# Routed tiles of an expert layer: register reads, gather buffers and result buffers of the tile loop

## What is computed

```python
def _L0_ffn_ref(x, router_w, w1, w2):
    ...
    logits = xt @ router_w.T
    probs = jax.nn.softmax(logits, axis=-1)
    top_w, top_i = lax.top_k(probs, K)
    e_sel = jnp.max(top_i, axis=-1)
    def step(out, inp):
        idx, W1e, W2e = inp
        y = jax.nn.silu(xt @ W1e) @ W2e
        mask = (e_sel == idx)[:, None]
        return (jnp.where(mask, y, out), None)
    ...
x = x + _L0_ffn_ref(_layernorm(x, axis=-1)[None], L0_ffn_router_w, L0_ffn_w1, L0_ffn_w2)[0]
```

## Time and profile before

| what | us |
|---|---|
| median of 3 runs | 2702.45 |
| lowest and highest run | 2683.28, 2715.99 |
| span of the profiled execution | 2680.6 |
| TensorE busy in it | 2412.7 (90%) |
| GpSimd busy in it | 799.4 (30%) |
| routed stage, from the first transpose to the issue of the last addition | 2532.82 to 2671.07 |

### The profile page before, as it was taken

The page is one execution under the profiler, slowest core; times in us unless marked ns, Lnnn a source line. Parts: engine busy times, 40 slices in busy tenths (PEclk is TensorE's granted clock), DMA queues, the critical chain, the costliest instruction groups (busy, mean ns, idle before and its releaser), DMA issues. The chain is left out here.

```text
span 2680.6 us, 44378 instructions
## 1 busy us (share of the span) xinstructions
PE 2412.7 (90%) x16483; PEld 1631.1 (61%) x16483; DVE 1387.3 (52%) x2865; ACT 800.5 (30%) x1093; POOL 799.4 (30%) x562
## 2 busy tenths in 40 slices
PE   5889899999999999998993999999998899999476
PEld 2676767676766666665562566666664556666354
DVE  6575858574676766765211444444440444444333
ACT  3333333332374554743111222222220011111132
POOL 2134444444555555555553000000000000000265
PEclk9889999999999999999996999999998999999698
DMA  9974545554313223123214566665646754444185
GB/s 388 396 252 126 163 93 158 138 149 111 95 1 60 25 35 59 0 60 77 54 1 134 212 218 217 217 217 217 217 156 222 248 179 168 166 163 147 44 159 112
DMA packets 160992, 392.23 MB, mean 146 GB/s; under 512 B 74064, under 2 KB 81082, under 8 KB 151260
## 3 DMA queue, kind: packets, MB, share of 16 engines
q1 hardware_dynamic: 77196, 299.90, 32.5%
q0 software_dynamic: 72864, 61.03, 13.0%
q10 hardware_dynamic: 10800, 29.50, 2.9%
HBM read 226.03 MB, written 169.81 MB: 148 GB/s over the span
## 5 line engine op out<-in xcount | busy, mean ns | idle before, releaser
L364 PE MATMUL pair<-arena 128*128 128x384 f16 (+2 forms) x5760 | 908.5, 319 | 26.9 <-SPq L353 7.4
L1761 PE MATMUL pair<-arena 128*128 128x384 f16 x4900 | 823.1, 328 | 66.9 <-issue 40.7
L675 POOL DMA_INDIRECT cells<-arena x392 | 640.7, 1634 | 641.7 <-DMA cells<-arena 467.5
L364 PEld LDWEIGHTS pair<-arena 128*128 128x128 f16 (+1 forms) x5760 | 568.2, 99 | 353.0 <-issue 30.1
L1761 PEld LDWEIGHTS pair<-arena 128*128 128x128 f16 x4900 | 476.8, 98 | 379.0 <-issue 59.6
L1586 PE MATMUL pair<-arena 128*128 128x256 f32 x600 | 172.5, 422 | 19.3 <-ACT arena L780 19.3
L705 POOL DMA_INDIRECT slots<-arena x25 | 29.2, 1167 | 517.0 <-DVEq L1460 501.0
L1597 PEld LDWEIGHTS pair<-arena 128*128 128x128 f32 x1200 | 157.1, 198 | 23.8 <-ACT arena L805 18.9
L1597 PE MATMUL pair<-arena 128*128 128x66 f32 x1200 | 157.3, 280 | 14.4 <-ACT arena L805 14.4
L1131 DVE SCALAR_TENSOR_TENSOR arena<-arena 128x256 f16<-128x256 f32 x392 | 161.8, 482 | 4.7 <-DVE arena L1056 4.4
L699 POOL TENSOR_TENSOR arena<-arena 128x128 f32<-128x128 f32 x24 | 12.2, 507 | 502.5 <-DMA arena<-cells 481.1
(11 more groups left out here) (194 smaller groups left out, 2266.6 us busy)
## 6 DMA issues: line engine op xcount, KB each, us to landing
cells<-arena POOLq DMA_DIRECT2D x25, 1600.0 KB, 11.8
arena<-cells SPq DMA_DIRECT2D x25, 1600.0 KB, 9.4
ahl_dram<-arena SPq DMA_DIRECT2D x25, 1600.0 KB, 12.8
arena<-ahl_dram SPq DMA_DIRECT2D x25, 1600.0 KB, 7.9
arena<-in_x SPq DMA_DIRECT2D x70, 384.0 KB
arena<-key_dram SPq DMA_DIRECT2D x28, 896.0 KB
split_w<-arena SPq DMA_DIRECT2D x32, 384.0 KB
arena<-split_w SPq DMA_DIRECT2D x32, 384.0 KB, 6.7
```

The source lines that it names most:

```text
L364: ins = nc.tensor.matmul(dst[half], left(k, a), right(k, b, half), start=start and n == 0, stop=stop and n == 2)
L675: nc.gpsimd.indirect_dma_start(cells, bass.IndirectOffsetOnAxis(ap=idx_all[:, m:m + 1], axis=0), val_all[:, m:m + 1], None, bounds_check=C ...
L1761: ins = nc.tensor.matmul(pair[u][:, half, 0:HD], a[:, 0, s * P:(s + 1) * P], X[part][:, s, half * HD:(half + 1) * HD], start=(s == 0 and p ...
```

## The change

Four things are altered, all in the routed stage, and nothing in what is computed.

1. TensorE reads three expert numbers before the first transpose. The number for tile 3 is read before `down(0)`; from there on the number for tile j+1 is read between `up(j-1)` and `down(j-2)` of step j.
2. There are six gather buffers (`NG`) instead of four. GpSimd issues six gathers first, and the gather for tile j+6 waits for the transposes of tile j.
3. There are four result buffers (`NO`) instead of two, so that `result(j)` waits for the addition of tile j-4. Two gathers and two additions count on semaphores of earlier phases, from the value that these have by then.
4. In the loop of GpSimd the addition for tile j stands ahead of the gather (for tile j+6) instead of behind it (for tile j+4). The clears write f32 instead of f16, over the same bytes of each buffer.

```diff
+NG, NO = 6, 4
...
-        g_in = [at(RX + D * u, 2 * D, dt=F16) for u in range(4)]
+        g_in = [at(RX + D * u, 2 * D, dt=F16) for u in range(NG)]
+        g_in32 = [at(RX + D * u, D) for u in range(NG)]
...
-        gathered, g_tr = [sem(f"gathered{u}") for u in range(4)], sem("g_tr")
+        gathered, g_tr = [sem(f"gathered{u}") for u in range(4)] + cleared, sem("g_tr")
+        gathered_base = [0] * 4 + [16 * ((T + 1 - u) // 2) for u in range(2)]
...
-        f_y, f_out, added = sem("f_y"), sem("f_out"), [sem("added0"), sem("added1")]
+        f_y, f_out, added = sem("f_y"), sem("f_out"), [sem("added0"), sem("added1"), far_st, scattered]
+        added_base = [0] * 2 + [16, 16 * ET_EDGES]
...
-            for u in range(4):
-                made.link(nc.gpsimd.memset(g_in[u], 0.0))
+            for u in range(NG):
+                made.link(nc.gpsimd.memset(g_in32[u], 0.0))
...
             def gather_rows(j):
                 pool.wait_ge(rows_ld[j % 4], 16 + 16 * (j // 4 + 1))
-                if j >= 4:
-                    pool.wait_ge(g_tr, j - 3)
+                if j >= NG:
+                    pool.wait_ge(g_tr, j - NG + 1)
...
-            for j in range(4):
+            for j in range(NG):
                 gather_rows(j)
             for j in range(FT):
-                if j + 4 < FT:
-                    gather_rows(j + 4)
                 add_rows(j)
+                if j + NG < FT:
+                    gather_rows(j + NG)
...
             def result(j):
                 dve.wait_ge(f_y, j + 1)
-                if j >= 2:
-                    dve.wait_ge(added[j % 2], 16 * (j // 2))
+                if j >= NO:
+                    dve.wait_ge(added[j % NO], added_base[j % NO] + 16 * (j // NO))
...
             pe.wait_ge(table, 1)
-            expert = [pe.value_load(expert_i[0:1, j:j + 1], min_val=0, max_val=NX - 1) for j in range(FT)]
-            rows_turn(0, 0, 0)
-            rows_turn(1, 1, 0)
+            expert = {}
+
+            def read_expert(j):
+                expert[j] = pe.value_load(expert_i[0:1, j:j + 1], min_val=0, max_val=NX - 1)
+
+            for j in range(3):
+                read_expert(j)
+            rows_turn(0)
+            rows_turn(1)
             pe.wait_ge(ffn_ready, 16 * (K + NX))
             up(0, 0)
-            rows_turn(2, 2, 0)
+            rows_turn(2)
             up(1, 1)
+            read_expert(3)
             down(0, 0)
-            rows_turn(3, 3, 0)
-            up(2, 0)
-            down(1, 1)
-            for j in range(4, FT):
-                rows_turn(j, j % 4, j // 4)
+            for j in range(3, FT):
+                rows_turn(j)
                 up(j - 1, (j - 1) % 2)
+                if j + 1 < FT:
+                    read_expert(j + 1)
                 down(j - 2, j % 2)
```

More of the change, by code:

```diff
@@ L236, in build @@
         lnb = at(RT + 19104, 2, 16)
-        g_in = [at(RX + D * u, 2 * D, dt=F16) for u in range(4)]
[L239 to L244, removed]
+        g_in = [at(RX + D * u, 2 * D, dt=F16) for u in range(NG)]
+        g_in32 = [at(RX + D * u, D) for u in range(NG)]
+        FR = RX + NG * D
+        fT = [[at(FR + HD * (2 * part + u), D, dt=F16) for u in range(2)] for part in range(2)]
+        hact = [at(FR + 1536 + P * u, P) for u in range(2)]
+        act_hi = [at(FR + 1792 + P // 2 * u, P, dt=F16) for u in range(2)]
+        act_lo = [at(FR + 1920 + P // 2 * u, P, dt=F16) for u in range(2)]
+        fo = [at(FR + 2048 + D * u, D) for u in range(NO)]
+        reach, reach_n = at(FR + 2048 + NO * D, FT, NX), at(FR + 2304 + NO * D, FT, NX)
         TAB = WST + 2304
@@ L324, in build @@
         edges_in, key_made, key_stored = sem("edges_in"), sem("key_made"), sem("key_stored")
-        cleared, scattered = [sem("cleared0"), sem("cleared1")], sem("scattered")
+        cleared, scattered = [sem(f"cleared{u}_then_gathered") for u in range(2)], sem("scattered_then_added")
         rows_ld = [sem(f"rows_ld{q}") for q in range(4)]
@@ L726, in add_rows @@
                 nc.gpsimd.indirect_dma_start(
-                    out, bass.IndirectOffsetOnAxis(ap=ids[:, j:j + 1], axis=0), fo[j % 2], None,
-                    bounds_check=NP - 1, oob_is_err=False, compute_op=ALU.add).then_inc(added[j % 2], 16)
-            for j in range(4):
+                    out, bass.IndirectOffsetOnAxis(ap=ids[:, j:j + 1], axis=0), fo[j % NO], None,
+                    bounds_check=NP - 1, oob_is_err=False, compute_op=ALU.add).then_inc(added[j % NO], 16)
+            for j in range(NG):
                 gather_rows(j)
             for j in range(FT):
-                if j + 4 < FT:
-                    gather_rows(j + 4)
                 add_rows(j)
-            for u in range(2):
-                pool.wait_ge(added[u], 16 * (FT // 2))
+                if j + NG < FT:
+                    gather_rows(j + NG)
+            for u in range(NO):
+                pool.wait_ge(added[u], added_base[u] + 16 * (FT // NO))
         @block.scalar
@@ L1874, in _, with rows_turn @@
             w_out_all = at(FW + 6192, NX * 2 * D, dt=F16)
-            def rows_turn(j, u, i):
-                q = u
-                pe.wait_ge(gathered[q], 16 * i + 16)
-                if reused(j):
+            def rows_turn(j):
+                q = j % NG
+                pe.wait_ge(gathered[q], gathered_base[q] + 16 * (j // NG) + 16)
+                if j:
                     pe.wait_ge(fT_hi, j)
```

8 lines of the change are left out of this document (4 added, 4 removed).

## The result

| | kernel before | changed kernel |
|---|---|---|
| median, us | 2698.84 (2683.28 to 2715.99, 4 runs) | 2662.61 (2661.11 to 2666.45, 4 runs) |
| ratio, 95% interval | | 0.9878 [0.9839, 0.9917] |
| span of the profiled execution, us | 2680.6 | 2661.0 |
| issue of the first gather, us from the span's start | 2518.28 | 2526.59 |
| from there to the first addition | 25.20 | 14.70 |

The kernel is 1.2% faster; the forecast was 2677, 1% faster, with a range from 2657 to 2697. The measured median lies 14 us under the forecast one, and a gain of over 1%, which came, had been given a chance of 0.44 against 0.53 for one within 1%. The four parts of the stage give 10.5 + 14.6 + 1.8 + 1.0 = 27.9 us. The spans of the two profiles are only 19.6 us apart, because the first gather came 8.3 us later in the changed one, in a part of the program that the change does not touch.

A forecast was written before the change was run, and what follows sets the result against it. The last stage's loop was taken as bound by a round trip of gathers and additions, at 4.27 us a step. Terms of -10.3 (start) and -15.3 (loop) sum to -25.6 us: median 2702.45 becomes about 2677, range 2657 to 2697.

The forecast's parts named there:

- Start: From first gather to first addition: 29 of 32 register reads leave the front, three are covered; term -10.3 us.
- The round trip through four gather buffers: Tile loop before: copy, addition, gather, transposes and products make a 12.9 us lap over three steps, 4.3 us each.
- The reads inside the loop: Between up and down products: nothing to 0.65 us exposed each, covered by TensorE's wait for gathers, taken at 0.
- Where the step comes to rest: Tile loop after: DMA engines 0.90 busy set 3.70 us a step, 100 us for 27 steps; term 15.3 us gained.
- rival B: Tile loop: DMA engines have headroom and GpSimd is the bound at 3.25 us a step; 2665 us, chance 0.25.
- TensorE still waiting for gathers: Tile loop: one of the signs that would show the forecast right; no size given.
- TensorE's wait ended by "issue" in each step: Tile loop: a sign that would show the forecast wrong, listed with the low clock under Rival C.
- Four result buffers: Result copies in the loop: 9.8 us of waits for additions go, counted in the step time and not again.
- End: From the 28th to the 32nd addition, 12.3 us before: equal within 1 us, and unchanged after the last addition.
- Rival A: Tile loop: DMA engines do not get fuller, step 4.1 to 4.27 us; 10 to 15 us gained, some 2690; chance 0.22.
- Rival C: Tile loop: reads hold TensorE at its low clock, steps 5.1 to 5.75 us; 2714 to 2732 us, chance 0.03.
- The Trainium skill's rule on latency under load: Gathers in the loop: HBM latency grows from 0.2 to 2 us; landing 5.91 would become 7.7, step 3.7.

The follow-up runs named there:

- experiment 10: Changed kernel with 17 of the 32 register reads in front of the first transpose and the other 15 behind the down products: 2665.26 us, ratio 0.984 to before.
- experiment 3: Changed kernel with only the reads moved: four gather and two result buffers and gather ahead of addition, as before the change: 2700.08 us.
- Experiment 1: Changed kernel with all 32 register reads in front of the first transpose again, new buffers and order kept: 2686.97 us.
- experiment 7: experiment 6 with four gather buffers instead of six, still four result buffers: 2696.98 us.
- experiment 4: Changed kernel with each step's register read behind the down products instead of ahead of them: 2678.94 us in a single run, later a median of 2668.82 us.
- experiment 6: experiment 4 with the gather ahead of the addition in GpSimd's loop, as before the change: 2666.42 us.
- experiment 5: experiment 4 with two result buffers instead of four: 2701.7 us.
- experiment 8: Changed kernel with each step's register read between the transposes and the up products: 2678.5 us.
- Experiment 9: Changed kernel with its register reads at the same place but without bounds on the number read: 2759.96 us.

## Why the prediction was right in its number, and where its steps failed

The sum, -25.6 us, was within 2.3 us of the 27.9 measured in the stage; the medians differed by 36.2 us in the first comparison and by 24.8 in the second (experiment 10), around that same 27.9. But two of its steps were wrong, in opposite directions, and it is luck that they cancelled.

- **Start: right.** "Term: -10.3 us" measured -10.5, and experiment 3 gives -10.3 to the reads alone. Experiment 1, with all 32 in front, brings the long start back.
- **What bound the kernel before: right.** The round trip through four gather buffers: put back in experiment 7, it gives 4.26 us a step, against 4.27.
- **"The reads inside the loop. ... On the chain I take it at 0": wrong**, and with it "the cover is TensorE's wait for gathers". TensorE's step is 3.73 - 2.65 = 1.08 us longer, above the upper bound of 0.65, and in the changed kernel TensorE is the chain. Taking the reads out gives 0.42 us a step (experiment 1), since GpSimd is next. The bound of 0.65 holds where a read is as short as on an idle TensorE: with reads of about 0.30 us the changed kernel's steps are 3.11 to 3.28, under the 3.30 of the prediction. What it left out is that the same read can last up to 1.19 us in the loop, and lasts 0.7 us or more in most steps. The cover was an inference from the kernel before, in which TensorE waited for gathers; the same change removes those waits, so the cover went with them. Its own sentence "without that cover the price would be 28 x 0.65 = 18 us" had the right shape.
- **"Where the step comes to rest. ... I estimate 0.90 busy": wrong in kind.** The 0.88 after is a result of the step, not its cause. Experiments 1, 4, 6 and 10 run the same traffic at 0.94 to 0.96 busy and 187 to 191 GB/s. With the read out of the way or at a better time the loop is at 3.31 to 3.38 us. In experiment 1 GpSimd has no idle time to speak of, so rival B's account was the better one; but 90 us of DMA work over 27 steps, 3.33 us, and TensorE's 3.2 with a read (experiment 6) lie so close to it that below 3.4 us no single bound can be named for all these kernels.
- **Why the number held: luck.** The step was forecast at 3.70 from the DMA engines and is 3.73 from TensorE. An overestimate of one resource stood where an underestimate of another belonged. The forecast's own signs separate them: "TensorE still waiting for gathers" did not come, and "TensorE's wait ended by 'issue' in each step" did.
- **"Four result buffers ... I count them in the step time and not again": undercounted.** 9.8 us of waits in the trace of before are the cost at 4.27 us a step. At 3.4 us a step two buffers cost 17 us, the 63.9 us of waits in experiment 5. The buffer count was necessary for the step, not a part of its gain.
- **Addition ahead of gather**: no effect (experiment 6).
- **End:** "equal within 1 us" measured -1.8, and another -1.0 after the last addition. The second goes with the result buffers: the three profiles with two of them (before, experiments 3 and 5) have 9.49 to 9.53 us there, all those with four 8.44 to 8.54.
- **Rival A: out**, the DMA engines do get fuller. **Rival C: out.** It had the read as the bound, but with the low clock; the clock was 1.00, and the gap of 1 us in every step did not lower it.
- **The Trainium skill's rule on latency under load** ("DMA: Bandwidth & Descriptors", section "Latency and other measured facts"): within the loop a gather's landing had a median of 5.2 us in experiment 7 at 153 GB/s (the profile of the kernel before gives no median), 5.7 in the changed kernel at 170, and 6.3 in experiment 1 at 191. It grows by 1.1 us, not 1.8. With six buffers no transpose of the changed kernel waits for it, and in experiment 1 the waits, 10.6 us, do not set the step.

Open: why the same read lasts 0.30 us at one time and up to 1.2 at another, and what lengthens the up products behind a read, by 0.1 us in the median in experiment 4 and by 0.4 in experiment 8 over the 1.26 of experiment 1. Experiment 9 was to narrow this down and did not.

## What to carry to other kernels

The cover that hides a moved instruction must be looked for in the kernel after the change: a wait which the same change removes hides nothing. A register read in an engine's stream is not free beside queued work: here it cost 0.3 us at the least and up to 1.3, by when it fell and not only by where it stood. So try it at each place of the step, and read how long the reads themselves last; where time is left in front that the engine would only wait through, put as many there as fit (experiment 10). And when a forecast comes out right, the waits must still name the bound that it named: here the remaining 10 us were found only because they named another.

## What the runs showed of the hardware that was not expected

- A register read on TensorE costs 0.65 us on an idle engine (record 301 ns). In the changed kernel's loop, behind 18 matmuls of 128 columns, its record is 297 to 1189 ns and the array stands 0.28 to 1.35 us for it, 1.08 us a step over the 2.65. Behind the six matmuls of the down products it costs 0.45 to 0.6 us. A second read right behind the first adds about 0.65 us again.
- The length of the read's record goes with how long ago GpSimd began to issue a gather, more than with the read's place in TensorE's stream; the table at the end of experiment 8 has the counts.
- The 18 up products take 1.17 us in the changed kernel, which reads ahead of the down products, a median of 1.26 us with no read in the loop (experiment 1), 1.36 in experiment 4 and 1.68 in experiment 8.
- A stretch of 27 steps at 0.96 of the DMA engines' time is reached by indirect gathers and accumulating additions; 187 to 191 GB/s is what they moved then, so a high share was no obstacle. The share is of packet times: the same 0.94 to 0.96 went with 187 in one kernel and 191 in another.
- The scatter of edges that ends long before this stage, 392 indirect DMAs one at a time, differs by tens of us between executions. In part 5 of the page of the profile its group has these rows, of the kernel before, the changed kernel and experiment 4 (busy us and mean ns, idle before and what ended most of it):

```profile
L675 POOL DMA_INDIRECT cells<-arena x392 | 640.7, 1634 | 641.7 <-DMA cells<-arena 467.5
```

```profile
L680 POOL DMA_INDIRECT cells<-arena x392 | 644.1, 1643 | 648.6 <-DMA cells<-arena 482.2
```

```profile
L680 POOL DMA_INDIRECT cells<-arena x392 | 655.9, 1673 | 660.1 <-DMA cells<-arena 481.6
```

Busy and idle together are 1282.4, 1292.7 and 1316.0 us, +10.3 and +33.6; the first gather of the last stage moves by +8.3 and +33.8. Over 14 profiles it lies between 2518.28 and 2556.05, and the shown profile of the kernel before has the earliest. That is why spans of single profiles (19.6 us apart) understate the change, and why the stage, which repeats within 0.3 us, was used to judge the experiments.
